# A graph and mixture-of-experts kernel: prelude and last stage rebuilt, and TensorE made to wait for its own signals in the layers

## What is computed

```python
def gcn_conv(x, edge_index, W, b, n_nodes):
    deg = segment_sum(ones, dst)
    norm = dinv[src] * dinv[dst]              # dinv = rsqrt(deg)
    h = x @ W.T
    return segment_sum(h[src] * norm[:, None], dst) + b
...
x = x + gcn_conv(relu(gcn_conv(layernorm(x), W1, b1)), W2, b2)
Xn = l2_normalize(layernorm(x));  sp = l2_normalize(slot_params, axis=1) * scale
logits = einsum('bmd,dnp->bmnp', Xn, sp)
D = softmax(logits, over nodes);  C = softmax(logits, over the 32 slots)
H = gelu(einsum('bnpd,ndh->bnph', einsum('bmd,bmnp->bnpd', Xn, D), W_down) + b_down)
x = x + einsum('bnpd,bmnp->bmd', einsum('bnph,nhd->bnpd', H, W_up) + b_up, C)
```

## Time and profile before

| what | us |
|---|---|
| median of three runs | 3285.74 (3274.72 to 3316.88) |
| the profiled execution: its time / its span | 3279.59 / 3277.7 |
| layer 1, from 233 to 1650 | 1417 |
| layer 2, from 1650 to 3064 | 1414 |
| busy share of the span: PE, DVE, ACT, POOL | 70%, 53%, 16%, 57% |

### The profile page before, as it was taken

How to read it: one execution, slowest core, us unless ns; L and a number is a source line. 1 busy time by engine, 2 the same in 40 slices (tenths; PEclk the granted TensorE clock), 3 DMA queues, 4 the chain that set the end, 5 groups by cost and what they waited for, 6 DMA issues and landing times.

```text
span 3277.7 us, 27906 instructions
## 1 busy us (share of the span) xinstructions
PE 2310.0 (70%) x8202; PEld 1417.6 (43%) x8203; DVE 1722.2 (53%) x2241; ACT 532.4 (16%) x981; POOL 1861.8 (57%) x1854
## 2 busy tenths in 40 slices
PE   7426766666777666667757768877777777777778
PEld 7413444444444444444424445544444444444334
DVE  7644555555555555555535545545555555555315
ACT  7730000000000000000101111111111111111210
POOL 3446666666666666666556666666666666666000
PEclk9998888888888888888878878888889888888889
DMA  9487877777778777777768888888788887888358
GB/s 319 160 349 265 272 263 262 265 255 263 260 269 278 263 266 266 259 256 263 241 223 292 302 279 271 298 275 278 268 286 290 283 297 272 290 282 286 133 167 350
DMA packets 240127, 877.90 MB, mean 268 GB/s; under 512 B 64344, under 2 KB 65128, under 8 KB 240060
## 3 DMA queue, kind: packets, MB, share of 16 engines
q0 software_dynamic: 143808, 666.65, 60.1%
q1 hardware_dynamic: 68580, 168.86, 14.2%
q10 hardware_dynamic: 27692, 41.82, 3.5%
HBM read 832.39 MB, written 82.00 MB: 279 GB/s over the span
## 4 chain that ended last, share of the span: by engine, by line
another core or an unknown queue 30%; issue 29%; PE 16%; DVE 13%; ACT 5%; DMA 3%; POOL 2%; DVEq 1%; ACTq 0%; SPq 0%; POOLq 0%
DVE acc L1013 7%; PE work L1243 5%; PE left L1227 5%; PE left L1278 2%; POOL rows L584 2%; DVE agg L1013 1%; ACT logits L673 1%; ACT xsT L662 1%; DVE agg L1051 1%; PE work L1258 1%; PE work L1235 1%; ACT dump L637 1%; DVE before_end L941 1%; DMA rows<-in_W_up 0%
## 5 line engine op out<-in xcount | busy, mean ns | idle before, releaser
L625 POOL DMA_INDIRECT rows<-table_layer,gidx x1764 | 1770.6, 1004 | 986.2 <-issue 505.7
L1227 PE MATMUL left<-rows,hot 128*128 128x384 f32 x2352 | 1008.6, 561 | 474.3 <-DVE agg L1051 359.9
L1013 DVE TENSOR_TENSOR acc<-acc,rows 128x768 f32<-128x768 f32 x1078 | 1037.8, 963 | 78.2 <-DMA rows<-table_layer,gidx 23.5
L1243 PE MATMUL work<-WT,aggT 128*128 128x384 f32 x2352 | 855.5, 509 | 105.6 <-ACT aggT L735 79.0
L1227 PEld LDWEIGHTS left<-rows,hot 128*128 128x128 f32 x2352 | 487.2, 219 | 794.0 <-issue 575.9
L1243 PEld LDWEIGHTS work<-WT,aggT 128*128 128x128 f32 x2352 | 467.3, 200 | 459.6 <-ACT aggT L735 103.8
L948 DVE TENSOR_TENSOR pick_col<-slot_of,fixed 128x6 f32<-128x6 f32 x49 | 7.9, 162 | 586.8 <-remote 563.6
L1235 PE MATMUL work<-ident,agg 128*128 128x128 f32 x588 | 127.7, 379 | 153.5 <-issue 109.4
L1026 DVE SCALAR_TENSOR_TENSOR xs<-work,dinv,xs 128x768 f32<-128x768 f32 x49 | 49.9, 1018 | 345.2 <-PE work L1243 261.7
L1235 PEld LDWEIGHTS work<-ident,agg 128*128 128x128 f32 x588 | 108.7, 205 | 219.1 <-issue 214.7
L741 ACT ACTIVATE ynext<-hid,dinv 128x768 f32<-128x768 f32 x49 | 45.8, 935 | 942.4 <-DVE hid L1021 923.9
(11 more groups left out here) (290 smaller groups left out, 1376.3 us busy)
## 6 DMA issues: line engine op xcount, KB each, us to landing
self_row<-table_layer SPq DMA_DIRECT2D x98, 384.0 KB
rows<-table_layer,gidx POOLq DMA_INDIRECT x1764
xstage<-in_x SPq DMA_DIRECT2D x71, 384.0 KB
xs<-in_x SPq DMA_DIRECT2D x60, 384.0 KB
table_layer<-ynext SPq DMA_DIRECT2D x49, 384.0 KB
xnew<-xs SPq DMA_DIRECT2D x49, 384.0 KB
table_layer<-xstage ACTq DMA_DIRECT2D x41, 384.0 KB
rows<-xnew SPq DMA_DIRECT2D x38, 384.0 KB, 3.9
```

The source lines that it names most:

```text
L625: pool.indirect_dma_start(rows[:, slot, :], None, table[l][0:ROWS, :], bass.IndirectOffsetOnAxis(ap=gidx[:, k % 2, slot:slot + 1], axis=0) ...
L1013: dve.tensor_tensor(acc[:, :, 0:H] if n < OWN - 1 else halves(agg[:, :]), acc[:, :, 0:H], halves(row), ALU.add).then_inc(S["added"], 1)
L1227: m = pe.matmul(left[:, h, 0:H], hot[:, b, c, :], rows[:, slot, h * H:(h + 1) * H], start=c == 0, stop=c == LEFT - 1)
L1243: m = pe.matmul(work[:, h, 0:H], aggT[:, kc, :], WT[l][:, kc, h * H:(h + 1) * H], start=kc == 0, stop=kc == KC - 1)
```

## The change

Three parts. **Prelude:** three more buffers (PARKED: both halves of `hot` and `before_end`) hold x tiles, so 32 instead of 35 are reloaded, and DVE waits for their stores before it first writes there. The clearing of the whole ring goes; four single slots are cleared behind the window gathers. The slot block moves in front of the window parts, on DVE and with its matmul on TensorE. The first DMA of dst no longer waits for a clearing, and the test of sortedness waits later. **Layers:** TensorE waits for six signals of its own. **Last stage:** 38 buffers, KEPT = 33, 19 loads ahead (8 of them in the last step); gains and first maximum of tiles 0 to 47 in front of the last scaling of the dense part; exponentials in thirds, that for cw inside the staging; the sum's matmul inside the mix loop; W_up's DMA earlier in SP's order. The new buffers of the last stage are twelve of the x stage instead of four, two of biases, one of row indices and two of logits. The core of the diff:

```diff
+PARKED = 3
+RELOADED = T - XBUFS - PARKED
 ...
-KEPT, TURNED, EARLY = 20, 5, 8
+KEPT, TURNED, EARLY, FIRST = 33, 5, 19, 8
+THIRDS = ((0, 16), (16, 32), (32, T))
 ...
+        parked = [hot[:, b, :, :].rearrange("p c n -> p (c n)") for b in range(2)] + [before_end[:, :]]
+
+        def x_buf(n):
+
+            if RELOADED <= n < RELOADED + PARKED:
+                return parked[n - RELOADED]
+            return xbuf[(n if n < RELOADED else n - PARKED) % XBUFS]
 ...
+                elif KEPT + TURNED - 2 <= n < KEPT + TURNED:
+                    sp.wait_ge(F["exp_in"], len(THIRDS) + 1)
 ...
-                        for n in range(EARLY):
+                        sp.wait_ge(S["idx_ready"], T)
+                        for n in range(FIRST):
                             load_tail(n)
 ...
+            for n in range(FIRST, EARLY):
+                load_tail(n)
             for b in range(2):
                 sp.wait_ge(L[1]["stored"][b], done_count(b, 2))
             for n in range(EARLY, T):
-                if n == KEPT - 4:
+                if n == EARLY + 8:
                     sp.wait_ge(L[1]["stats_done"], T)
                     sp.wait_ge(L[1]["logit_read"], T)
+                if n == KEPT + TURNED:
+                    sp.dma_start(wup, a["W_up"].rearrange("n h d -> h n d")).then_inc(F["w_in"], 16)
                 load_tail(n)
-            sp.dma_start(wup, a["W_up"].rearrange("n h d -> h n d")).then_inc(F["w_in"], 16)
             for n in range(T, out_load(T)):
 ...
-            pool.memset(flat, 0.0).then_inc(s["ring_clear"], 1)
             last_anchor = pool.to_reg(ANCHORS - 1)
-            pool.wait_ge(s["ring_clear"], 1)
 ...
+            uncleared = [SLOT["left", c] for c in range(LEFT) if SLOT["left", c] * D >= 2 * wide]
+            for slot in uncleared:
+                pool.memset(rows[:, slot, :], 0.0).then_inc(s["ring_clear"], 1)
+            pool.wait_ge(s["ring_clear"], len(uncleared))
 ...
+            token_roots(T - 1, T, 2)
+            for g, (t0, t1) in enumerate(THIRDS):
+                act.wait_ge(F["exp_in"], g + 1)
+                act.activation(dw[:, t0:t1, :], dw[:, t0:t1, :], ACT.Exp).then_inc(F["exp_done"], 1)
+            for t in range(T):
+                if t == 0:
+                    act.wait_ge(F["exp_done"], len(THIRDS))
+                if t >= 4:
                     act.wait_ge(F["mixed_done"], t - 3)
-                act.activation(w_tile[:, k % 4, :], dw[:, ds(t, 1), :], ACT.Copy, scale=coef[:, ds(t, 1)]
+                act.activation(w_tile[:, t % 4, :], dw[:, t, :], ACT.Copy, scale=coef[:, t:t + 1]
                                ).then_inc(F["w_staged"], 1)
-            act.wait_ge(F["exp_done"], 1)
-            load_sweep(act, stage_w)
+                if t == THIRDS[1][1]:
+                    act.wait_ge(F["exp_in"], len(THIRDS) + 1)
+                    act.activation(cw[:, :, :], cw[:, :, :], ACT.Exp).then_inc(F["exp_done"], 1)
 ...
+            dve.tensor_scalar(iota_ps, iota_row[:, :], -1.0, float(P), ALU.mult, ALU.add).then_inc(s["fixed_ready"], 1)
+            dve.tensor_copy(pick_iota, iota_row[:, 0:EXTRA]).then_inc(s["fixed_ready"], 1)
+            one.then(dve.tensor_scalar(norm2_kq, norm2_kq, L2_EPS, None, ALU.add))
+            one.then(dve.reciprocal(norm2_kq, norm2_kq))
+            one.then(dve.tensor_scalar(norm2_kq, norm2_kq, scale_col, None, ALU.mult))
+            for n in range(EXPERTS):
+                q = slice(n * SLOTS_PER, (n + 1) * SLOTS_PER)
+                one.mark(dve.tensor_tensor(sp_c[:, :, q], sp_c[:, :, q], norm2_kq, ALU.mult))
+            dve.wait_ge(one.sem, one.n)
+            dve.sem_inc(s["slots_scaled"], 1)
+            dve.wait_ge(s["slot_sums"], 1)
+            one.then(dve.tensor_scalar(norm2[:, 0:SLOTS], mm[:, 1, 0:SLOTS], 1.0 / D, None, ALU.mult))
+            one.then(dve.tensor_tensor(sp_c[:, :, :], sp_c[:, :, :],
+                                       norm2[:, 0:SLOTS].unsqueeze(1).to_broadcast([P, KC, SLOTS]), ALU.subtract))
+            dve.sem_inc(s["slots_ready"], 1)
 ...
+                    for m in range(PARKED):
+                        dve.wait_ge(y_out[m], 16)
                     mark_ends(0)
 ...
+                def token_gains(c0, c1, nth):
+                    dve.wait_ge(S["stats_done"], c1)
+                    rv, cf = recip_var[:, c0:c1], coef[:, c0:c1]
+                    one.then(dve.tensor_scalar(rv, ssq[:, c0:c1], 1.0 / D, LN_EPS, ALU.mult, ALU.add))
+                    one.then(dve.reciprocal(rv, rv))
+                    one.then(dve.tensor_tensor(cf, ssq[:, c0:c1], rv, ALU.mult))
+                    dve.sem_inc(F["root_in"], 1)
+                    dve.wait_ge(F["root_done"], 2 * nth)
+                    one.then(dve.tensor_scalar(cf, cf, L2_EPS, None, ALU.add))
+                    one.then(dve.reciprocal(cf, cf))
+                    one.then(dve.tensor_tensor(cf, cf, rv, ALU.mult))
+                    dve.wait_ge(S["logit_read"], c1)
+                    one.then(dve.tensor_tensor(logits[:, c0:c1, :], logits[:, c0:c1, :],
+                                               cf.unsqueeze(2).to_broadcast([P, c1 - c0, SLOTS]), ALU.mult))
 ...
+                                token_gains(0, T - 1, 1)
+                                one.then(dve.tensor_reduce(top, logits[:, 0:T - 1, :].rearrange("p t q -> p q t"),
+                                                           AX.X, ALU.max))
                             scale_dense()
 ...
-            dve.wait_ge(L[1]["stats_done"], T)
-            dve.wait_ge(L[1]["logit_read"], T)
-            for b in range(2):
-                dve.wait_ge(L[1]["stored"][b], done_count(b, 2))
-
-            one.then(dve.tensor_scalar(recip_var[:, 0:T], ssq[:, :], 1.0 / D, LN_EPS, ALU.mult, ALU.add))
-            one.then(dve.reciprocal(recip_var[:, 0:T], recip_var[:, 0:T]))
-            one.then(dve.tensor_tensor(coef, ssq[:, :], recip_var[:, 0:T], ALU.mult))
-            dve.sem_inc(F["root_in"], 1)
-            dve.wait_ge(F["root_done"], 2)
-            one.then(dve.tensor_scalar(coef, coef, L2_EPS, None, ALU.add))
-            one.then(dve.reciprocal(coef, coef))
-            one.then(dve.tensor_tensor(coef, coef, recip_var[:, 0:T], ALU.mult))
-            gain = coef.unsqueeze(2).to_broadcast([P, T, SLOTS])
-            one.then(dve.tensor_tensor(logits[:, :, :], logits[:, :, :], gain, ALU.mult))
-
-            top = small[:, 0, 0:SLOTS]
-            one.then(dve.tensor_reduce(top, logits[:, 0:T - 1, :].rearrange("p t q -> p q t"), AX.X, ALU.max))
+            token_gains(T - 1, T, 2)
 ...
+            for t0, t1 in THIRDS:
+                one.then(dve.tensor_tensor(dw[:, t0:t1, :], logits[:, t0:t1, :],
+                                           top.unsqueeze(1).to_broadcast([P, t1 - t0, SLOTS]), ALU.subtract))
+                dve.sem_inc(F["exp_in"], 1)
 ...
                     m.then_inc(S["left_found"], 1)
+                    pe.wait_ge(S["left_found"], t + 1)
 ...
                             m.then_inc(S["left_summed"], 1)
+                            if c % 2:
+                                pe.wait_ge(S["left_summed"], LEFT * t + c + 1)
 ...
                             m.then_inc(S["agg_turned"], 1)
+                            pe.wait_ge(S["agg_turned"], t)
 ...
                                 m.then_inc(S["dense_done"], 1)
+                                pe.wait_ge(S["dense_done"], t)
 ...
                             m.then_inc(S["x_turned"], 1)
+                            pe.wait_ge(S["x_turned"], t)
 ...
                             m.then_inc(S["logit_done"], 1)
+                            pe.wait_ge(S["logit_done"], t)
 ...
-            pe.wait_ge(F["sumd_ready"], 1)
-            pe.matmul(tp[0:SLOTS, 0, 0:1], small[:, 2, 0:SLOTS], ones[:, 0:1], start=True, stop=True
-                      ).then_inc(F["sumd_done"], 1)
 ...
+                if t == KEPT:
+                    pe.wait_ge(F["sumd_ready"], 1)
+                    pe.matmul(tp[0:SLOTS, 0, 0:1], small[:, 2, 0:SLOTS], ones[:, 0:1], start=True, stop=True
+                              ).then_inc(F["sumd_done"], 1)
```

More of the change, by code:

```diff
@@ L40 @@
 X_LANES = 6
-RELOADED = T - XBUFS
+PARKED = 3
+RELOADED = T - XBUFS - PARKED
 STAT_GROUP = 4
@@ L402, in build @@
                      + [flat[:, b * D:(b + 1) * D] for b in range(4)]
-                     + [ffn[:, EXPERTS * D + T * SLOTS:(EXPERTS + 1) * D + T * SLOTS]])
+                     + [ffn[:, EXPERTS * D + T * SLOTS:(EXPERTS + 1) * D + T * SLOTS]]
+                     + [logits[:, :, :].rearrange("p t q -> p (t q)")[:, b * D:(b + 1) * D] for b in range(2)])
         def mix_buf(t):
@@ L661, in _ @@
                     act.wait_ge(x_in[t % X_LANES], 16 * (t // X_LANES + 1))
-                    act.activation(sum_dump[:, t % STAT_GROUP, :], xbuf[t % XBUFS], ACT.Copy,
+                    act.activation(sum_dump[:, t % STAT_GROUP, :], x_buf(t), ACT.Copy,
```

(19 more changed lines are left out.)

70 lines of the change are left out of this document (23 added, 47 removed).

## The result

| | us | |
|---|---|---|
| kernel before | 3280.23 | 3271.19 to 3316.88 |
| changed kernel | 3399.01 | 3383.24 to 3415.35 |
| ratio | 1.034 | 95% interval 1.024 to 1.044 |

The changed kernel is slower by 119 us. The time lies inside the range, but not on the forecast's 3300: the ends gained what was worked out, the layers lost nearly three times what was.

The account below looks back on a forecast made before the run. POOL's gather issue, 23.6 us a tile, was taken as the layers' floor, with late TensorE signals behind waits above it. From 3279.6: −15 prelude, −26 last stage, +60 layers gave 3298.6, written as 3300; range 2850 to 3430.

Parts of the forecast that it names:

- Prelude: Before the first table gather: ring clearing removed and slot block hidden in DVE idle time, −15 us, bounds −11 and −17.
- Layers: Both layers: TensorE's waits for its own signals cost +60 us, bounds +25 and +100, all of it in layer 2.
- Last stage: After the layers: earlier gains, earlier w_tile staging, earlier W_up and fewer tiles read back, −26 us, bounds −18 and −32.
- steps 1 and 2: Last stage: gains and first maximum into DVE idle time, −4.5 us; earlier w_tile staging, −5.6, subtracting in thirds one more.
- The wait for W_up: Last stage, before L1284: moving W_up's DMA earlier cuts TensorE's 10.01 us stand to 3 us, −7.
- experts and output loop together: Last stage: 38 buffers let 13 fewer tiles be read back in the output loop, −8 us, bounds −2 and −12.
- hold stays: Layers, the forecast itself: signals stay held and TensorE's own waits end with the hold; 3250 to 3390, chance 0.36.
- Layer 1: find_left's wait delays later matmuls, but slack before L1051 absorbs it: 0, bounds 0 and +2.7 us a tile.
- agg_turned's wait: Layer 2: chunk 1's matmuls move behind the hold, delaying dense matmuls; 0.9 to 2.3 us where it strikes, +60 in all.
- Signals are released: Rival, layers: TensorE's own waits let held signals out, pick_col and aggT start 5.7 us earlier; 2809, half 3024; chance 0.31.
- TensorE itself is held: Rival, chunk 3 of layer 1: TensorE stands through POOL's burst, clock restarts low, +2 to +4 us a tile; 3400–3600; chance 0.19.
- The waits do nothing: Rival, layers: the own-signal waits have no effect and only the ends count; 3239, bounds 3230 to 3250; chance 0.14.

## Why the prediction was right or wrong

3399 lies inside 2850 to 3430, but partly by luck. The range was drawn wide enough for the rivals; the forecast's own, 3250 to 3390, does not hold it, and of the three classes it was the least likely that came, slower by more than 2% (0.26). By the prediction's own sign it was wrong, too: the period of a tile was not to be over 30 us, and from 28.9 it went to 30.6 (2831 + 170 us for 98 tiles).

**Prelude**, −15 (−11 to −17): measured −16.3. The clearing is gone and the slot block hidden, and nearly the whole upper bound came. The four small clears took 2.78 us together, behind the window gathers, near the 0.65 each that were estimated.

**Last stage**, −26 (−18 to −32): measured −25.2, and term by term. (The bounds of its terms add up to −20 and −30; −18 and −32 are 2 us wider.) From the last scaling to the first mixing matmul before 24.2 us (3059.09 to 3083.29), after 13.3, so −10.9 for the −11.1 of steps 1 and 2. The wait for W_up:

```profile
3226.03 2.77 PE L1315 MATMUL left<-slot_iota,w_tile 128*32 128x384 f32 x4 [3.82 <-ACT w_tile L795]
...
3294.27 0.73 PE L1325 MATMUL work<-ident,agg 32*128 32x32 f32 x6 [3.03 <-DVEq L1147]
```

3.03 us in front of the first expert matmul instead of 10.01: −7.0, the number forecast. From the first mixing matmul to this one it is 75.0 before and 68.2 after, −6.7, and from there to the end 119.5 and 111.8: −7.7, experts and output loop together, for which −8 stood.

**Layers**, the step that failed: +60 (+25 to +100) against +170 in the traces. The mechanism was in part the forecast's, "hold stays": pick_col's waits were nearly unchanged and TensorE waited for itself with several microseconds each. Its other sign, aggT's waits unchanged, did not come (263 us to 24), and logit_done came later than without the waits. Two terms were mis-sized.
- Layer 1 was taken at 0. I had seen that L1021 would be about 2 us late, and put it into TensorE's slack. In the trace after, pick_col starts at 1064.96 and the scaling (now L1067) at 1071.43, 6.5 us behind it; in the earlier trace rows 4.35. The 2.1 us came, and what made them was the clock, which was counted in layer 2 and in the rival but not here. At the 0.34 us a record of the prediction the last third of the dense part would have ended at 1040.6, in time for the 1040.80. But behind its stand of 4.86 us TensorE's granted clock was 0.50 (1.2 GHz) from 1065 to 1068, and chunk 3's four matmuls took 2.93 us instead of 1.54, the eight dense ones behind them 3.32 instead of 2.74. The tile became 0.8 us longer: +38 to +41 us by the runs. The upper bound given for it, 2.7 a tile, held.
- Layer 2 was costed by agg_turned's wait alone, +60. In the changed kernel TensorE stands behind the transposes in 2 places, 17 us in all; behind the logit matmuls it stands in 45, 346 us in all. The wait behind logit_done, which comes last in the tile, was named in the change and given no price but a restart of 0.3 us. Alone it costs +142, all waits of the layer together +116 to +119. Without it the other five kinds cost +72; that this is near the +60 says little for the term, since those five are not taken apart. The row to cost it from was in the same tile: what comes behind it is chunk 0, from which POOL gets its next slots, and all 397 us of POOL's pauses there end with TensorE's sums. I asked what a held signal does to the engine that needs it, and not, for each wait, which of TensorE's work stands behind it and who is fed by that.

**The rivals.** "Signals are released" did not happen: of pick_col's 563 us of waits 504 are still there. Its number, 2809, is near the kernel before in other jobs (2810 to 2816), where the signals are in time without any wait, but by chance: it contains the 41 us of the ends, and the changed kernel takes 2772 there. "TensorE itself is held" was worked out for chunk 3 of layer 1, 2 to 4 us a tile; layer 1 gave 0.8, while TensorE was held in layer 2, by another signal. Its lower end, 3400, is where the kernel landed, by that other place. "The waits do nothing", 3239, is right for the ends alone (3236 to 3246), and the waits do nothing only where signals are in time.

## What to carry to other kernels

A wait of an engine for its own signal cost nothing here while signals came at once, and 0.8 us a tile in layer 1 and 2.4 in layer 2 where they were 5 and 7 us late. Cost each by what stands behind it in that engine's order, above all by work that frees buffers for the gathers. Where an engine waits for two signals, take which one ended the wait from the counts in the program; here the profile's name for it was wrong in the rows that mattered. Slack read from a table of waits belongs to all edits together, and may be gone with the first. And run a pair in several jobs before calling a change good or bad: this one is 3.4% slower in one condition and 1.4% faster in the other, while the ends without the waits are faster in both (0.984 and 0.988).

## What was not expected of the hardware

TensorE's signals have two conditions. In one they are seen 0.03 to 0.04 us after the matmul (1017.61 to 1017.64), in the other mostly 4 to 7 us later while POOL issues gathers, in single places over 10. The same kernel on the same chip took 2816.07 us in one job and 3280.07 in another, and all thirteen and seven runs of these jobs stayed with their time. In the rows of the kernel before, late left_found and agg_turned are seen when POOL pauses, in 72 of 74 places, but late logit_done in the middle of a burst in 25 of 34; so the pause is not the whole rule, and nothing here tested it. What decides between the two conditions, and whether the lateness alone makes the tile 28 us long, stays open.
